# Pair scans over neighbouring decays, with part of the decays in SBUF, in a selective-scan and FFN kernel

## The reference

```python
u = silu(conv3(x))
B, C = split(u @ W_bc + b_bc)                     # 16 states each
dt = softplus((u @ W_dt + b_dt) @ W_dtp + b_dtp)
h[l] = exp(A * dt[l]) * h[l-1] + dt[l] * x[l] * B[l]     # h[-1] = 0 in each sequence
y[l] = sum over states of C[l] * h[l]  + x[l] * Dcoeff
x = layernorm(x + y)
x = layernorm(x + fp4_linear(silu(fp4_linear(x, Wg)) * fp4_linear(x, Wu), Wd))
```

## Time and profile before

| | |
|---|---|
| median of three runs | 330.97 us (330.10 to 331.23) |
| the profiled execution | 329.99 us |
| its span, first to last instruction | 328.2 us |
| mean granted TensorE clock | 0.953 of full speed |
| busy: DVE, POOL, PE, ACT | 298.6, 261.0, 259.0, 244.6 us |

### The profile page before, as it was taken

One profiled execution on the slowest core, in us unless ns is written; L12 is line 12 of the kernel. 1 busy time (PEld: TensorE's weight loads), 2 busy tenths in 40 slices (PEclk: granted clock), 3 DMA queues, 4 the chain that ended last, 5 costly groups with the idle time before them and its releaser, 6 DMA issues.

```text
span 328.2 us, 3994 instructions
## 1 busy us (share of the span) xinstructions
PE 259.0 (79%) x1158; PEld 127.7 (39%) x1158; DVE 298.6 (91%) x329; ACT 244.6 (75%) x527; POOL 261.0 (80%) x147
## 2 busy tenths in 40 slices
PE   2766959687863998978898888879794959887994
PEld 1222412223321344533444435334441436436684
DVE  3869986899999999999999999999999799998973
ACT  2477885965895589698879888888888495656584
POOL 0076763569558999899999999999999988995771
PEclk9979897879998799999999999999999797999999
DMA  2690380840075000822074206510561000100003
GB/s 40 154 211 23 82 187 22 176 112 0 0 160 130 1 2 15 194 48 64 0 161 98 64 3 142 113 32 2 113 144 32 3 0 0 32 3 1 0 8 89
DMA packets 19261, 21.85 MB, mean 67 GB/s; under 512 B 6112, under 2 KB 15144, under 8 KB 19240
## 3 DMA queue, kind: packets, MB, share of 16 engines
q1 hardware_dynamic: 18520, 21.05, 28.2%
q10 hardware_dynamic: 720, 0.56, 0.9%
HBM read 2.72 MB, written 2.10 MB: 15 GB/s over the span
## 4 chain that ended last, share of the span: by engine, by line
POOL 41%; issue 16%; DVE 15%; PE 13%; ACT 7%; SPq 4%; DMA 1%; POOLq 0%; DVEq 0%; ACTq 0%
POOL product L901 20%; POOL qh_norm L948 5%; DVE states L1182 5%; DVE db L1162 4%; POOL qh_magic L928 3%; POOL qh_norm L923 3%; SPq L514 3%; POOL dtx L909 2%; POOL qx_norm L934 2%; ACT L560 1%; POOL qx_magic L928 1%; ACT ps_decay L570 1%; PE ps_prep L1507 1%; PE ps_f L1605 1%; POOL qx_norm L923 1%
## 5 line engine op out<-in xcount | busy, mean ns | idle before, releaser
L901 POOL TENSOR_TENSOR product<-states,c_rep 128x1024 f32<-128x1024 f32 x59 | 128.1, 2186 | 22.1 <-DVE states L1182 21.5
L570 ACT ACTIVATE ps_decay<-dt_rep,aneg 128x512 f32<-128x512 f32 x128 | 86.8, 691 | 27.5 <-DVE states L1182 19.4
L1182 DVE TENSOR_TENSOR_SCAN states<-ps_decay,db 128x512 f32<-128x512 f32 x64 | 74.9, 1201 | 0.3
L1162 DVE SCALAR_TENSOR_TENSOR db<-ps_b,bbc_rep,dt_rep 128x2048 f32<-128x2048 f32 x31 | 72.1, 2327 | 2.5 <-PE ps_b L1526 1.6
L1182 DVE TENSOR_TENSOR_SCAN states<-ps_decay,states,db 128x512 f32<-128x512 f32 x54 | 66.6, 1261 | 3.7 <-ACT ps_decay L570 3.7
L1526 PE MATMUL ps_b<-u_feat,wbc_rep 128*128 128x512 f32 x64 | 36.8, 659 | 5.9 <-DVE db L1162 5.1
L1520 PE MATMUL ps_prep<-u_feat,wbc_rep 128*128 128x512 f32 x56 | 34.4, 698 | 8.6 <-ACT c_rep L646 8.6
L560 ACT ACT_TABLE_LOAD x26 | 33.4, 1283 | 0.5
L1484 PE MATMUL ps_y<-product,gather 128*32 128x512 f32 x248 | 31.9, 608 | 0.0
L1568 PE MATMUL ps_f<-gate_t,xq_t 128*128 128x352 f32 x48 | 18.7, 514 | 8.7 <-ACT hidden L653 7.0
L1507 PE MATMUL ps_prep<-x_feat,tap_diag 128*128 128x512 f32 x42 | 21.2, 640 | 3.8 <-DMA x_feat<-in_L_attn_x 2.5
(11 more groups left out here) (256 smaller groups left out, 494.9 us busy)
## 6 DMA issues: line engine op xcount, KB each, us to landing
dt_rep<-dtx SPq DMA_DIRECT2D x124, 128.0 KB, 2.4
x_tok<-in_L_attn_x SPq DMA_DIRECT2D x8, 256.0 KB, 2.9
out<-y_out SPq DMA_DIRECT2D x7, 256.0 KB, 2.3
dt_rep<-dtx ACTq DMA_DIRECT2D x4, 128.0 KB, 3.7
out<-y_out SPq DMA_DIRECT2D x2, 128.0 KB, 1.8
hidden<-in_L_ffn_w_down SPq DMA_DIRECT2D x1, 176.0 KB, 3.6
x_feat<-in_L_attn_x SPq DMA_DIRECT2D x8, 0.5 KB, 2.2
hidden<-in_L_ffn_w_gate SPq DMA_DIRECT2D x1, 128.0 KB, 3.3
```

The source lines that it names most:

```text
L570: nc.scalar.activation(ps_decay[BANK_OF[i]][:], dt_rep[p][:, c, 0, :], ACT.Exp, scale=aneg[:, c, m:m + 1]).then_inc(decay_done, 1)
L901: nc.gpsimd.tensor_tensor(in_turn(product[:, j % PRODUCTS]), in_turn(groups(s, 2 * j, 2)), in_turn(over(c_rep[p][:, j // SET_PAIRS, :], 2) ...
L1162: nc.vector.scalar_tensor_tensor(out=db[m % DB][:], in0=over(ps_b[:], QUADS), scalar=bbc_rep[:, 0, m:m + 1], in1=dt_rep[p][:, :, 1, :], op ...
L1182: nc.vector.tensor_tensor_scan(out=groups(s, k, 1)[:, 0, :], data0=ps_decay[BANK_OF[s.at(GROUPS, k)]][:], data1=db[k // QUADS % DB][:, k % ...
```

## The change

Four things are changed.

- The decays go into five places in place of three: PSUM banks 0 and 1, now one tensor of two neighbouring halves (`ps_pair`), bank 2, and two neighbouring rows in SBUF (`decay_rows`, called `ROW_A` and `ROW_B`). Even units write groups 0 and 1 of every four to the PSUM pair and groups 2 and 3 to the SBUF pair. Odd units go round bank 2, bank 0 and `ROW_A`; the last group of the last unit takes `ROW_B`.
- Even units scan two groups in one operation of 1024 columns (`scan`). The first decay column of the second group is kept at zero (set once by two memsets; `decay` writes only columns 1 to 511 of that half), so that the state starts again there. Odd units scan group by group as before, as each needs its own initial state. Decays of even units are issued two at a time.
- After the first unit, in even units, POOL's product takes a whole set (four groups, 2048 columns) in one operation (`by_sets`) in place of two of 1024.
- `qh_magic` on DVE moves from slot 8 to slot 11; in the first step the halo load goes between the second and the third quarter of `replicate` in place of behind the fourth, and `dtx` is named at slot 5 in place of 6. The waits of the late FFN matmuls follow the new banks.

`by_sets` reads `s.first % 2 == 0 and s.beyond(1)`, so unit 0 keeps products of two groups, and units 2, 4 and 6 take sets.

```diff
+ROW_A, ROW_B = DECAYS, DECAYS + 1
 def bank_of(unit, k):
-    return 1 if unit == UNITS - 1 and k == GROUPS - 1 else (GROUPS * (unit - UNITS + 1) + k) % DECAYS
+    if unit % 2 == 0:
+        return (0, 1, ROW_A, ROW_B)[k % 4]
+    return ROW_B if unit == UNITS - 1 and k == GROUPS - 1 else (2, 0, ROW_A)[k % 3]
...
-    "dve h quant": {0: (1, False), 1: (4, False), 2: (5, True), 5: (8, False)}, "pool x norm": 3, "pool xq": 8,
+    "dve h quant": {0: (1, False), 1: (4, False), 2: (5, True), 5: (11, False)}, "pool x norm": 3, "pool xq": 8,
...
-    "act C": (7, 8, 9, 11), "pool dtx": 6,
+    "act C": (7, 8, 9, 11), "pool dtx": 5,
...
+def by_sets(s):
+    return s.first % 2 == 0 and s.beyond(1)
...
+        decay_rows = sb("decay_rows", [128, 2, UNIT])
...
-        ps_decay = [pb(f"ps_decay{j}", [128, UNIT]) for j in range(DECAYS)]
+        ps_pair = pb("ps_pair", [128, 2, UNIT])
+        ps_decay = [ps_pair[:, 0, :], ps_pair[:, 1, :], pb("ps_decay2", [128, UNIT])[:]]
+        decays = ps_decay + [decay_rows[:, n, :] for n in range(2)]
+        pairs = {0: ps_pair, ROW_A: decay_rows}
...
-                if a is not None:
+                if a is not None and not s.beyond(1):
+                    replicate(a, 1 - p, (0, 1))
+                    load_halo(b, p)
+                    replicate(a, 1 - p, (2, 3))
+                elif a is not None:
                     replicate(a, 1 - p)
-                if b is not None:
+                if b is not None and s.beyond(1):
                     load_halo(b, p)
...
-                nc.scalar.activation(ps_decay[BANK_OF[i]][:], dt_rep[p][:, c, 0, :], ACT.Exp,
+                start = 1 if s.first % 2 == 0 and k % 2 else 0
+                nc.scalar.activation(decays[BANK_OF[i]][:, start:], dt_rep[p][:, c, 0, start:], ACT.Exp,
                                      scale=aneg[:, c, m:m + 1]).then_inc(decay_done, 1)
...
-                    if at:
+                    if at and at[0].first % 2:
                         decay(*at)
+                    elif at and k % 2 == 0:
+                        for n in range(2):
+                            decay(*later(s, a, k, AHEAD + n, p))
...
-                pool.wait_ge(scan_done, s.at(GROUPS, 2 * j + 2))
+                n = 2 if by_sets(s) else 1
+                pool.wait_ge(scan_done, s.at(GROUPS, 2 * (j + n)))
...
-                    if s is not None and k % 2 and (a is not None or k < GROUPS - QUADS):
+                    if by_sets(s) and k % QUADS == QUADS - 1:
+                        times_c(s, k // 2 - 1, p)
+                    elif not by_sets(s) and k % 2 and (a is not None or k < GROUPS - QUADS):
                         times_c(s, k // 2, p)
...
+                if p:
+                    nc.vector.tensor_tensor_scan(
+                        out=groups(s, k, 1)[:, 0, :], data0=decays[bank], data1=of[:, k % QUADS, :],
+                        initial=states[0][:, k, UNIT - 1:UNIT], op0=ALU.mult, op1=ALU.add).then_inc(scan_done, 1)
+                else:
+                    nc.vector.tensor_tensor_scan(
+                        out=groups(s, k, 2).rearrange("p g t -> p (g t)"),
+                        data0=pairs[bank][:].rearrange("p g t -> p (g t)"),
+                        data1=of[:, k % QUADS:k % QUADS + 2, :].rearrange("p g t -> p (g t)"),
+                        initial=0.0, op0=ALU.mult, op1=ALU.add).then_inc(scan_done, 2)
...
-                gate_free = ((xq_evac, f.at(1, 1)), (db_done, UNITS * SETS), (scan_done, before_last + 15),
+                gate_free = ((xq_evac, f.at(1, 1)), (db_done, UNITS * SETS), (scan_done, before_last + 13),
...
-                up_free = ((y_done, f.at(1, -1)), (scan_done, before_last + 13), (scan_done, before_last + 16),
+                up_free = ((y_done, f.at(1, -1)), (scan_done, before_last + 14), (scan_done, before_last + 13),
```

More of the change, by code:

```diff
@@ L900, in times_c @@
                     pool.wait_ge(sum_done, s.at(SETS, (j - PRODUCTS) // SET_PAIRS + 1))
-                nc.gpsimd.tensor_tensor(in_turn(product[:, j % PRODUCTS]), in_turn(groups(s, 2 * j, 2)),
-                                        in_turn(over(c_rep[p][:, j // SET_PAIRS, :], 2)),
-                                        ALU.mult).then_inc(product_done, 1)
+                to = product[:, j % PRODUCTS:j % PRODUCTS + n].rearrange("p j g t -> p (j g) t")
+                nc.gpsimd.tensor_tensor(in_turn(to), in_turn(groups(s, 2 * j, 2 * n)),
+                                        in_turn(over(c_rep[p][:, j // SET_PAIRS, :], 2 * n)),
+                                        ALU.mult).then_inc(product_done, n)
             def dtx_of(a, o):
@@ L1041, in _ @@
             setup.mark(nc.vector.memset(qx.amax[:], 1.0))
+            setup.mark(nc.vector.memset(ps_decay[1][:, 0:1], 0.0))
+            setup.mark(nc.vector.memset(decay_rows[:, 1, 0:1], 0.0))
             setup.mark(nc.vector.memset(x_square[:, TILES * D // BLOCK, :], 0.0))
@@ L1176, in scan @@
                     dve.wait_ge(product_done, s.at(PAIRS, (k - ring - GROUPS) // 2 + 1))
-                dve.wait_ge(decay_done, s.at(GROUPS, k + 1))
+                groups_here = 1 if p else 2
+                dve.wait_ge(decay_done, s.at(GROUPS, k + groups_here))
                 if k < 2 and not s.beyond(1):
@@ L1181, in scan @@
                     dve.wait_ge(db_done, s.at(SETS, k // QUADS + 1))
-                nc.vector.tensor_tensor_scan(
-                    out=groups(s, k, 1)[:, 0, :], data0=ps_decay[BANK_OF[s.at(GROUPS, k)]][:],
-                    data1=db[k // QUADS % DB][:, k % QUADS, :],
-                    initial=states[0][:, k, UNIT - 1:UNIT] if p else 0.0,
-                    op0=ALU.mult, op1=ALU.add).then_inc(scan_done, 1)
+                bank, of = BANK_OF[s.at(GROUPS, k)], db[k // QUADS % DB]
+                if p:
[8 more added lines that the diff above has]
+                        initial=0.0, op0=ALU.mult, op1=ALU.add).then_inc(scan_done, 2)
             def gate(f, slot, early):
@@ L1262, in step @@
                     for early in (True, False):
-                        if not early and s is not None:
+                        if not early and (p or k % 2 == 0):
                             scan(s, k, p)
```

## The result

The changed kernel takes 363.34 us (median; 362.67 to 363.86) beside 331.10 us for the kernel before on the same chip: a ratio of 1.1014 (1.0974 to 1.1055; the two medians alone give 1.097), 10% slower. The forecast was 371 us (338 to 390), slower with a chance of 0.88. The profiled execution took 362.67 us with a span of 360.9, so the span grew by 32.7 us, and 36.7 us of busy time came on POOL and 30.3 on DVE, while PE got 9.4 (its mean granted clock was 0.936 of full speed, 0.953 before) and ACT 0.6.

A forecast was written before the change was run, and what follows sets the result against it. DVE and POOL were taken as both full in steady steps. Start -2.5, SBUF-scan costs across the units less unit 0's scan saving, and end -0.5 gave +41.8 on 329.99, or 371.8; 371 us was taken, range 338 to 390.

The forecast's parts named there:

- The step that decides: SBUF-decay scans and POOL's operations exclude each other both ways: +7.9 us per even step, +7 per odd one; chance 0.74.
- The rival without contention: SBUF scans beside products take the PSUM scan's time, leaving only the savings: 327 us (322 to 331); chance 0.12.
- Falling in step: Rival: POOL stands idle waiting for the SBUF pair just when it is scanned: 345 us (336 to 354); chance 0.12.
- The size of the steps: Cost of SBUF scans per unit step: +7.9 us in units 4 and 6, +14 for units 3 and 5 together.
- the set's product: POOL's merged product in even units from unit 2: 4.24 us, saving 0 to 0.06 us each, 12 times: nothing.
- Time goes with columns: POOL's product time was taken as proportional to columns within 0.06 us, from 2.12 us for 1024 and `dtx`'s 1.09 for 512.
- floor for even steps: POOL's even step: 33.05 us own work plus 4 x 2.16 held by SBUF pair scans, 41.7 us.
- walk: One step followed through DVE's and POOL's queues with the forecast durations: 41.2 us for an even step, 41.3 for an odd one.
- DVE's waits: In odd steps five SBUF scans each wait 1.07 us for the rest of a POOL operation, 5.4 us in all.
- Pair scans: Two groups per DVE scan in even units: 2.16 us a pair, 0.08 saved each, 2.6 us in all (0 to 5.1).
- Sets and slot 11: Sets save nothing; `qh_magic` at slot 11 is covered and costs nothing, or up to 2 us a step if POOL is early.
- The start's term: Earlier halo load and `dtx` let the convolution start at about 46 us; 2.5 us gained, at most DVE's 3.67.

The follow-up runs named there:

- the separate run: A kernel of its own with only scans and products, apart and side by side; beside products six pair scans take 13.20 us from PSUM, 22.76 from SBUF.

## Why the prediction was right

**Contention.** The step that decides was right in mechanism. Scans from SBUF and POOL's operations take turns, whichever issues first goes first, and PSUM scans are untouched. The Trainium skill, page "SBUF — State Buffer", section "Who interferes with whom", has the second to issue blocked entirely until the first is done; the traces agree in both directions, the one that no row of before showed as well (4.85 us for a POOL operation of 2.86). The rival without contention falls with 366 us for one SBUF bank alone. Falling in step falls as a main course: POOL is busy for 37.6 to 39.2 us of the steps of units 3 to 6, and lengths of SBUF pairs spread from 2.23 to 4.78 us. One part of that rival came true: no set's product is held (all twelve take 3.87 to 3.89 us), since it starts when its last pair is scanned. In even units it is the FFN's operations, and in unit 6 `dtx`, that are held.

**The size of the steps.** Against the forecast's +3.7, +5, +7, +7.9, +7, +7.9 and +5 for units 1 to 7 stand 1.9, 4.3, 5.3, 5.8, 6.2, 6.6 and 3.6: each was 0.7 to 2.1 us too dear, 9.8 of 43.5 us in all.

In even steps the term that was mis-sized is the set's product: it was put at 4.24 us, and its pitch is 3.83 (194.41 to 198.24 above), so four sets take 1.6 us less of POOL. "Time goes with columns" had compared a product with `dtx`, which is another operation: a product of 512 columns takes 1.26 us in the separate run, not 1.09. The holds were sized nearly right: in unit 4 `hq`, `qx_norm` (twice) and `qh_norm` take 4.58, 3.05, 3.15 and 4.85 us, 2.0 each over their shortest, against 2.16. 33.05 + 4 x 2.0 - 1.6 = 39.4 is the step of unit 4; the 40.3 of unit 6 hold 2 us of idle POOL. The forecast's floor for even steps, 41.7, was no floor: its own walk gave 41.2.

In odd steps DVE's waits were mis-sized. The five SBUF scans of unit 3 take 2.30, 2.23, 2.43, 1.68 and 1.25 us, 3.6 more than 1.26 each, where 5.4 had been put down; the held `qh_magic` takes 2.41 in place of 0.57. 33.85 + 3.6 + 1.8 = 39.3 of the step of 39.7. For units 1, 2 and 7 no run tells the terms apart.

**Pair scans.** 2.18 us was the pitch in the kernel (163.38 to 165.56 in unit 4) and 2.20 in the separate run, against a forecast of 2.16: 0.06 us saved per pair, 2 us in all, lost under the rest.

**Sets and slot 11.** Put at nothing, which is wrong where there are no SBUF decays: the sets cost 2.4% there (7.3 us of it in the three even steps) and slot 11 another 0.7% (0.9882 to 1.0119 to 1.0190), in each case because `qh_magic` meets a product. The price of 2 us for a `qh_magic` that is held was named, and in the odd steps of the changed kernel it is right (2.41 us in place of 0.57); what failed is that it was also called covered, and that a longer product lengthens that hold was missed.

**The start and the end.** The start's term, -2.5, was too small by itself: 3.7 us at unit 1's second set and 1.2% of the time, its upper end. In the changed kernel the scans in SBUF took part of it back at once: `dtx` was held (2.60 us), and against the start alone the copies start at 37.62 in place of 34.54, the halo follows at 42.69 in place of 39.56, and the convolution at 47.19 in place of 45.88 (the forecast had 46). With unit 0's scans -1.2 was forecast and -2.1 came. At the end -0.5 was forecast and +1.1 came; the last scan, from `ROW_B`, takes 3.03 us beside POOL's `qh` codes:

```profile
320.32 3.66 POOL L952 TENSOR_TENSOR qh_magic<-qh_norm,qh_magic 128x1408 bf16<-128x1408 f32 x1
...
322.03 3.03 DVE L1213 TENSOR_TENSOR_SCAN c_rep<-decay_rows,states,db 128x512 f32<-128x512 f32 x1
```

**The sum by the runs.** In parts of the time before: start -1.2%, sets +2.4%, slot 11 +0.7%, SBUF decays with the pair scans +8.2% (7.8 by the two medians); together +10.1%. These are prices in this order, and the last one holds some 3 us either way of who came first in units 0 and 1.

**The number.** The sum of +41.8 stood on the profiled execution and gave 371.8 us; +32.7 and 362.67 came: 9.8 too dear in the steps and 0.9 at the start, 1.6 too cheap at the end. So the errors are mostly of one sign, and the time came in below the sum and inside the range. One reading was wrong without weight: POOL is second by busy time and not third.

## What to carry to other kernels

Before an input of a streaming operation moves from PSUM to SBUF, look whether another engine works in SBUF all the time beside it: the operation alone may cost the same (2.2 us here) and both engines still lose its whole length. A hold of this kind has no idle time in the profile; look for one instruction whose records spread by the length of a neighbour, and count a neighbour that is merged into a longer one as a longer hold. Where a decay, or any input made ahead, goes round few buffers, look at the turn between loops: one buffer too late stops all that the in-order producer has queued behind it.

## What the hardware showed beyond that

- A product on POOL has a part that does not grow with its columns: 512, 1024 and 2048 columns take 1.26, 2.16 and 3.86 us in the kernel's order of elements. The order counts too: group by group they take 1.26, 2.34 and 4.49.
- A bf16 operation of DVE that reads one SBUF tensor is held as well: `qh_magic` 3.35 us behind a set's product, 0.70 without, and 2.18 behind a product of two groups.
- Who comes first can hang on a third engine: with TensorE's granted clock at 0.50 in place of 0.86 for a microsecond, one scan of unit 0 came 0.7 us later, lost its turn, and with a second lost turn unit 1 was 3.0 us late, with the same instructions.
